# Input rows of the routed expert tiles: gathered and turned by TensorE, or scattered to slots in DRAM and turned by VectorE

## The reference, cut to what matters

```python
def _moe_forward(hidden_states, gate_w, expert_gate, expert_up, expert_down, shared_gate, shared_up, shared_down):
    x = hidden_states.reshape(-1, hdim)                       # 2048 x 512, after a layer norm
    probs = jax.nn.softmax(x @ gate_w.T, axis=-1)             # 8 experts
    routing_weights, selected = jax.lax.top_k(probs, 2)
    routing_weights = routing_weights / (routing_weights.sum(axis=-1, keepdims=True) + 1e-20)
    combine = ...                                             # 2048 x 8, two entries a row
    out = jax.nn.silu(x @ shared_gate.T) * (x @ shared_up.T) @ shared_down.T
    g = jnp.einsum('nh,eih->nei', x, expert_gate)             # i = 352
    u = jnp.einsum('nh,eih->nei', x, expert_up)
    y = jnp.einsum('nei,ehi->neh', jax.nn.silu(g) * u, expert_down)
    return out + jnp.einsum('neh,ne->nh', y, combine)
```

## Time and profile before

| | us |
|---|---|
| median of 3 runs | 1586.21 |
| lowest and highest | 1584.1, 1586.29 |
| span of the profiled execution | 1583.3 |

### The profile page before, as it was taken

One profiled execution on the slowest core, in us unless ns is written; L12 is line 12 of the kernel. 1 busy time (PEld: TensorE's weight loads), 2 busy tenths in 40 slices (PEclk: granted clock), 3 DMA queues, 4 the chain that ended last, 5 costly groups with the idle time before them and its releaser, 6 DMA issues.

```text
span 1583.3 us, 23811 instructions
## 1 busy us (share of the span) xinstructions
PE 1556.1 (98%) x7776; PEld 1332.6 (84%) x7777; DVE 1040.8 (66%) x2230; ACT 583.5 (37%) x997; POOL 455.2 (29%) x390
## 2 busy tenths in 40 slices
PE   7999999999999999999999999999999999999996
PEld 5888888888888888888888888888888889999995
DVE  4798877788887788787787778755663582222221
ACT  4444443434444434444344344333111322333332
POOL 3445332134223233222233221113200003332342
PEclk9999999999999999999999999999999999999998
DMA  7886764677976686985686777466631037778743
GB/s 288 280 315 221 231 220 138 236 289 263 307 278 225 249 307 242 305 302 211 247 308 248 298 295 277 138 212 194 235 100 48 7 114 217 233 194 264 220 86 40
DMA packets 106004, 351.70 MB, mean 222 GB/s; under 512 B 11248, under 2 KB 31728, under 8 KB 100400
## 3 DMA queue, kind: packets, MB, share of 16 engines
q1 hardware_dynamic: 92688, 312.63, 54.9%
q0 software_dynamic: 13216, 37.79, 10.2%
HBM read 227.18 MB, written 123.19 MB: 221 GB/s over the span
## 4 chain that ended last, share of the span: by engine, by line
PE 93%; DVE 3%; DMA 1%; POOL 1%; issue 1%; ACT 1%; POOLq 0%; SPq 0%; ACTq 0%; DVEq 0%
PE bank L366 30%; PE bank L368 30%; PE bank L367 30%; PE bank L1956 1%; PE bank L2075 1%; DMA rows<-x_rows,ids_e 0%; DMA resid<-x 0%; POOL store L669 0%; PE bank L2032 0%; DMA out<-x_early,ids_e 0%; DVE place_hot L1638 0%; DVE tile_vals L1648 0%; DVE resid L1476 0%; PE bank L1756 0%; PE bank L1755 0%
## 5 line engine op out<-in xcount | busy, mean ns | idle before, releaser
L711 POOL TENSOR_TENSOR probs<-probs,causal 128x256 f32<-128x256 f32 x126 | 90.7, 740 | 408.5 <-ACT probs L891 408.5
L368 PE MATMUL bank<-store,wqk 128*128 128x512 f32 x512 | 202.1, 395 | 0.0
L367 PE MATMUL bank<-store,wqk 128*128 128x512 f32 x512 | 201.8, 394 | 0.0
L366 PE MATMUL bank<-store,wqk 128*128 128x512 f32 x512 | 201.8, 394 | 0.0
L1284 DVE SCALAR_TENSOR_TENSOR resid<-bank,factor,resid 128x512 f32<-128x512 f32 x256 | 189.3, 741 | 1.2 <-PE bank L368 1.1
L669 POOL TENSOR_TENSOR pre_split<-pre_raw,pre_split 128x1528 fp32r<-128x1528 f32 x34 | 120.7, 3550 | 142.4 <-ACT pre_split L853 142.4
L889 ACT ACTIVATE probs<-bank 128x512 f32<-128x512 f32 x189 | 85.8, 528 | 131.2 <-PE bank L368 131.2
L368 PEld LDWEIGHTS bank<-store,wqk 128*128 128x128 f32 x512 | 96.0, 188 | 22.9
L367 PEld LDWEIGHTS bank<-store,wqk 128*128 128x128 f32 x512 | 96.0, 188 | 20.8
L366 PEld LDWEIGHTS bank<-store,wqk 128*128 128x128 f32 x512 | 96.0, 188 | 20.0 <-DMA wqk<-wqk_parts 0.2
L1315 DVE TRANSPOSE_TENSOR_REDUCE bank<-probs 128x16 f32<-128x512 f32 (+3 forms) x256 | 108.4, 492 | 0.0
(11 more groups left out here) (333 smaller groups left out, 3966.9 us busy)
## 6 DMA issues: line engine op xcount, KB each, us to landing
pre_parts<-pre_split SPq DMA_DIRECT2D x34, 1528.0 KB, 6.6
wqk<-wqk_parts SPq DMA_DIRECT2D x96, 512.0 KB, 5.0
pre_raw<-pre SPq DMA_DIRECT2D x34, 764.0 KB, 8.0
store<-wv_parts SPq DMA_DIRECT2D x12, 2048.0 KB, 9.4
wo<-wo_parts SPq DMA_DIRECT2D x48, 512.0 KB, 8.3
expert_w<-pre_parts SPq DMA_DIRECT2D x8, 2816.0 KB, 11.6
wqk_parts<-wqk SPq DMA_DIRECT2D x16, 1024.0 KB, 5.1
expert_w<-pre_parts SPq DMA_DIRECT2D x8, 1536.0 KB, 8.8
```

Source lines behind the costliest of these rows:

```text
L366: nc.tensor.matmul(out_ap, a_hi, b_hi, start=first, stop=False)
L367: nc.tensor.matmul(out_ap, a_hi, b_lo, start=False, stop=False)
L368: return nc.tensor.matmul(out_ap, a_lo, b_hi, start=False, stop=last)
L711: nc.gpsimd.tensor_tensor(diagonal, diagonal, causal[:, :, :], ALU.mult).then_inc(S["masked"], 1)
```

## The change

- A new DRAM tensor `es` holds the 39 tiles in slot order. It is filled with zeros by SP in five pieces of up to 2 MB in the attention units 7 to 11.
- As soon as `slot_e` is there, POOL scatters the layer-normed rows of all 16 tiles to their two slots, 32 indirect DMAs (`scatter_e`). Their source is SBUF: SP first reloads the rows from `x3_rows` into `resid` (whose own tiles have been stored by then) and a new buffer `staging`, in four loads (`stage`).
- The first six tiles of the routed stage are gathered by row number as before, `gather(0)` to `gather(3)` after 22 of the scatters, `gather(4)` and `gather(5)` after 26.
- Tiles 6 to 38 are loaded from `es` by four DMAs of 64 KB each, issued by ScalarE in step `g-4` between `y_copy_e` and `aT_high`. VectorE turns tile `g` in step `g-2`, between `xT_low` and `aT_low`. TensorE no longer transposes them.
- The weight loads wait for the end of the up and of the down product (`e_up`, `e_y`) instead of for the transposes that follow them.

```diff
-        E_ROWS, E_AHEAD = 4, 6
+        E_ROWS, E_GATHERED, E_LOADS = 4, 6, 4
+        STAGED = ((0, 6), (6, 10), (10, 13), (13, 16))
+        GATHERS_FROM, MORE_GATHERS = 11, 13
...
-            fills = [(xs, "zero_filled_x", at) for at in range(0, XTILES, ZTILES)]
+            fills = [(xs, "zero_filled_x", at) for at in range(0, XTILES, ZTILES)] + [(es, "zero_filled_e", at) for at in range(0, ETILES, 2 * ZTILES)]
...
-                for part, used, lo, n in (("up", "e_xT_ready", 0, UP), ("down", "e_aT_ready", UP, DOWN)):
+                for part, used, lo, n in (("up", "e_up", 0, UP), ("down", "e_y", UP, DOWN)):
...
-                        sp.wait_ge(S[used], tiles_before + 1)
+                        sp.wait_ge(S[used], tiles_before)
...
+            def stage(n):
+                lo, hi = STAGED[n]
+                to = staging[:, :, :] if n == 1 else resid[:, lo % 10:lo % 10 + hi - lo, :]
+                sp.dma_start(to, x3_rows[lo * P:hi * P].rearrange("(t p) d -> p t d", p=P)).then_inc(S[f"x_tile{n}"], 16)
...
+            def scatter_e(t):
+                if t in dict(STAGED):
+                    pool.wait_ge(S[f"x_tile{[lo for lo, _ in STAGED].index(t)}"], 32)
+                for c in range(TOPK):
+                    nc.gpsimd.indirect_dma_start(es, bass.IndirectOffsetOnAxis(slot_e[:, c, t:t + 1], 0), staged(t), None).then_inc(scat[min(t // 3, 2)], 16)
...
-            pool.wait_ge(S["ids_ready"], 1)
-            for g in range(E_AHEAD):
-                gather(g)
+            pool.wait_ge(S["slots_ready"], TOPK)
+            for t in range(TILES):
+                if t == GATHERS_FROM:
+                    pool.wait_ge(S["ids_ready"], 1)
+                    for g in range(E_ROWS):
+                        gather(g)
+                if t == MORE_GATHERS:
+                    for g in range(E_ROWS, E_GATHERED):
+                        gather(g)
+                scatter_e(t)
             pool.wait_ge(S["stored"], 16 * TILES)
             for g in range(ETILES):
-                if g + E_AHEAD < ETILES:
-                    gather(g + E_AHEAD)
                 add_rows(g)
...
+            def load_turned_e(g):
+                if g == E_GATHERED:
+                    for n, tiles in enumerate((3, 3, TILES - 6)):
+                        act.wait_ge(scat[n], SCAT_X + 16 * TOPK * tiles)
+                if g >= E_GATHERED + E_ROWS:
+                    act.wait_ge(S["e_xT_ready"], g - E_ROWS + 1)
+                if g >= E_GATHERED + 2:
+                    act.wait_ge(S[f"x3_turned{g % 2}"], TURNED_X3 + 16 * QUADS * ((g - E_GATHERED) // 2))
+                load_turned(resid[:, g % E_ROWS, :], es[g * P:g * P + P], S[f"x3_turned{g % 2}"], nc.scalar)
...
+            def turn_e(g):
+                dve.wait_ge(S["e_xT_lo"], g)
+                dve.wait_ge(S[f"x3_turned{g % 2}"], TURNED_X3 + 16 * QUADS * ((g - E_GATHERED) // 2 + 1))
+                turn(resid[:, g % E_ROWS, :]).then_inc(S["e_xT_ready"], 1)
...
-                    transpose_rows_e(i, j + 1)
+                    if rows_next:
+                        transpose_rows_e(i, j + 1)
```

More of the change, by code:

```diff
@@ L154, in build, with staged @@
         tile_vals = sb("tile_vals", [P, TOPK * TILES, 3 * ETABLE], F32R)
+        staging = sb("staging", [P, 4, D])
+        assert sb.at <= second_region + 4 * 2 * KC * SH_WIDTH
+        def staged(t):
+            return staging[:, t - 6, :] if 6 <= t < 10 else resid[:, t % 10, :]
         NE = EXPERTS * TILES
@@ L340, in build @@
         SH_PIECES = 2 * (2 * KC + 4)
-        E_ROWS, E_AHEAD = 4, 6
+        E_ROWS, E_GATHERED, E_LOADS = 4, 6, 4
+        STAGED = ((0, 6), (6, 10), (10, 13), (13, 16))
+        GATHERS_FROM, MORE_GATHERS = 11, 13
+        SCAT_X = 16 * BATCH
+        TURNED_X3 = 16 * 4 * (TILES - TURNED_FROM) // 2
         LAST_PARTS = ((0, SEQ), (SEQ, SEQ), (2 * SEQ, 2 * P))
@@ L374, in every, with load_turned @@
             return row.rearrange("p (m k) -> p k m", k=KC)[:, k, :]
-        def load_turned(tile, source, done):
+        def load_turned(tile, source, done, engine=nc.sync):
             for r in range(QUADS):
-                nc.sync.dma_start(tile[r * BLOCK:(r + 1) * BLOCK, :].rearrange("x (a q) -> x a q", a=QUADS),
+                engine.dma_start(tile[r * BLOCK:(r + 1) * BLOCK, :].rearrange("x (a q) -> x a q", a=QUADS),
                                   source[:, r * P:(r + 1) * P].rearrange("(a x) q -> x a q", x=BLOCK)).then_inc(done, 16)
@@ L546, in _ @@
                     rows_of, done, at = fills[u - 2]
-                    fill(rows_of, done, at, min(ZTILES, rows_of.shape[0] // P - at))
+                    fill(rows_of, done, at, min(ZTILES if done == "zero_filled_x" else 2 * ZTILES, rows_of.shape[0] // P - at))
                 if u == 2 + len(fills):
@@ L560, in _ @@
                     load_ct(1)
-            sp.wait_ge(S["zero_filled_x"], 16 * len(fills))
+            sp.wait_ge(S["zero_filled_x"], 16 * -(-XTILES // ZTILES))
+            sp.wait_ge(S["zero_filled_e"], 16 * -(-ETILES // (2 * ZTILES)))
             def load_row(ph, source, g, j):
@@ L644, in _ @@
             turn_x3(TILES - 1)
+            def stage(n):
+                lo, hi = STAGED[n]
+                to = staging[:, :, :] if n == 1 else resid[:, lo % 10:lo % 10 + hi - lo, :]
+                sp.dma_start(to, x3_rows[lo * P:hi * P].rearrange("(t p) d -> p t d", p=P)).then_inc(S[f"x_tile{n}"], 16)
             for t in range(TILES):
+                if t == 6:
+                    for j in range(2):
+                        sp.wait_ge(S[f"x3_stored{j}"], 16 * (TILES // 2))
+                    sp.wait_ge(S["stored"], 16 * t)
+                    stage(0)
+                    sp.wait_ge(S["s_up"], 2 * TILES)
+                    stage(1)
+                if t == 11:
+                    sp.wait_ge(scat[0], SCAT_X + 16 * TOPK * 3)
+                    stage(2)
+                if t == 12:
+                    sp.wait_ge(scat[1], SCAT_X + 16 * TOPK * 3)
+                    stage(3)
                 if t == TILES - 2:
@@ L1020, in step_e @@
                         y_copy_e(g - 1)
+                if E_GATHERED <= g + E_LOADS < ETILES:
+                    load_turned_e(g + E_LOADS)
                 if g == 0:
@@ L1163, in route_slots @@
                 link(nc.vector.tensor_reduce(w.slot_f[:, :], w.above[:, 0:NE].rearrange("p (e t) -> p t e", e=EXPERTS), mybir.AxisListType.X, ALU.add))
-                link(nc.vector.tensor_copy(slot_e[:, c, :], w.slot_f[:, :]))
+                nc.vector.tensor_copy(slot_e[:, c, :], w.slot_f[:, :]).then_inc(S["slots_ready"], 1)
+                dve.wait_ge(S["slots_ready"], c + 1)
             def route_tiles(w, tiles, tile_expert):
@@ L1490, in step @@
                     shared_add(TILES - 1)
+                if ph == "e" and E_GATHERED <= g + 2 < ETILES:
+                    turn_e(g + 2)
                 if between:
@@ L2076, in transpose_rows_e, with e_step @@
                 last.then_inc(S["e_xT_ready"], 1)
-            def e_step(i, j, first=False, second=True):
+            def e_step(i, j, first=False, second=True, rows_next=False):
                 g = 4 * i + j
@@ L2120, in _ @@
             pe.wait_ge(S["s_y_out"], TILES)
-            e_step(0, 1, second=False)
-            by_fours(pe, e_step, 2, ETILES - 2)
+            e_step(0, 1, second=False, rows_next=True)
+            for g in range(2, E_GATHERED - 1):
+                e_step(g // 4, g % 4, rows_next=True)
+            by_fours(pe, e_step, E_GATHERED - 1, ETILES - 2)
             last = ETILES - 1
-            transpose_rows_e(last // 4, last % 4)
             e_down(last - 2, place(last - 2), True)
```

4 lines of the change are left out of this document (3 added, 1 removed).

## The result

The changed kernel took **1607.31 us** (1605.94 to 1609.27), against 1586.25 before in the same comparison: a ratio of 1.0138, interval 1.0127 to 1.015. It is slower by 1.4%. The forecast was 1590, with a range up to 1604. The profiled execution has a span of 1607.2, 23.9 above that of before.

A forecast was written before the change was run, and what follows sets the result against it. TensorE, busy for 98% of the span, was taken as the bound. On a span of 1583.3: +6.9 front, +3.5 clock, -15.5 transposes, +9.0 late loads gives 1587.2; plus 2.9 to the median, 1590 us, range 1577 to 1604.

The forecast's parts named there:

- the chain of adds: Routed stage: each add waits for the last one's landing; no term in the sum, only a rival of chance 0.13.
- The gain on TensorE: Tiles 6 to 38: four row transposes leave each of 33 steps, 6.74 to 6.27 us, -15.5 us in all.
- The front: Start of the routed stage: 22 scatters ahead of the first gather make row 0 late, +6.9 us, ends 4.1 and 10.
- The issue: Front: after 22 scatters at 1.27 us each, gather 0 goes out at 1301.3, 4.1 us later than before.
- The landing: Front: gather 0, under expert 1's weights, lands 8.5 us after its issue, against 5.71 before.
- The clock: Front: TensorE idles some 7 us and its granted clock drops, +3.5 us, bounds 0 and 4.
- The loads against the weights: Six weight pairs in the routed stage: turned loads land 1.5 us late in each, +9 us, ends 0 and 24.
- rival A: Routed stage: turned loads are in time, perhaps through several pieces per engine turn; 1581 us, chance 0.28.
- 32 turns x 17.5 / 32: Turned load beside a weight pair: its 32 pieces per engine alternate with weight packets over the pair's 17.5 us.
- ScalarE's issues: Routed steps: four DMA issues at 0.45 to 0.67 us each, nothing on the path; rival if over 0.74, chance 0.10.
- Rival B: End of the routed stage: the chain of adds, each awaiting the last landing, sets the end; 1586 to 1591, chance 0.13.
- The median: Whole kernel: the measured median lies 2.9 us above the profiled execution's span, so 1587.2 becomes 1590 us.

The follow-up runs named there:

- e1: The changed kernel with its adds going in turn to three tensors, two thirds of the results left out of the output: 1591.83 us.
- e17: The changed kernel with scatters spread and 14 tiles gathered as in e14, weights unpaced, adds to three tensors (two thirds of results left out): 1570.94 us.
- e11: The changed kernel with ten tiles gathered, gathers 0 to 3 after 14 scatters, expert 1's weights after the scatters, later weights over three steps: 1601.58 us.
- e3: The changed kernel with only an eighth of the weights of experts 2 to 7 loaded, results wrong: 1607.3 us.
- e13: e11 with the 32 scatters writing only the first 16 of a row's 512 floats, to another tensor, results wrong: 1600.64 us.
- e14: The changed kernel, 14 tiles gathered, at most 16 scatters before the first add, others behind adds 0 to 7, later weights over three steps: 1582.68 us.
- e5: The changed kernel with every expert weight load issued as four, each a quarter of the columns, same bytes: 1610.21 us.
- e9: The changed kernel with the weights of experts 2 to 7 spread over three steps, same bytes: 1600.98 us.
- e16: e14 with the later weights spread over four steps instead of three: 1579.36 us.

## Why the prediction was wrong

**The step that failed: the chain of adds stood in the sum at nothing.** The sum took it as running beside TensorE. By the profiled spans, the front took 17.3 us up to the second add (10.4 forecast), 33 steps that are 0.50 shorter would give 16.5 (15.5 forecast), the turned loads cost nothing (9 forecast), and the chain of adds, with the stalls that it causes, takes what remains: 23.9 - 17.3 + 16.5 = 23.1 us (nothing forecast). e1 puts it at 25 and e17 at 26.7. The terms one by one:

**The gain on TensorE: right.** Steps of 6.24 where it isn't held up (e1, e17); I had 6.27.

**The front: right in kind, half the size.** I had +6.9 for row 0; it was 15.7. Two terms failed. The issue: 1301.3 forecast, 1306.0 measured, since the scatters are not 0.97 us each while VectorE works on the routing tables. POOL's timeline of the changed kernel at the start of them:

```profile
1273.08 1.06 POOL L831 DMA_INDIRECT es<-resid,slot_e  x1 [104.63 <-DVE slot_e L1221]
1274.45 0.97 POOL L831 DMA_INDIRECT es<-resid,slot_e  x1 [0.30 <-issue]
1275.72 2.10 POOL L831 DMA_INDIRECT es<-resid,slot_e  x1 [0.30 <-issue]
1278.13 0.96 POOL L831 DMA_INDIRECT es<-resid,slot_e  x1 [0.30 <-issue]
1279.40 2.60 POOL L831 DMA_INDIRECT es<-resid,slot_e  x1 [0.30 <-issue]
```

Six of the first twelve took 1.2 to 2.6 us, and none of the later ones did; VectorE was busy for 35.24 of the 40 us from 1260. The Trainium skill, "SBUF — State Buffer", section "SBUF: two separate sides", says that GpSimd can't write the descriptors of its DMAs while VectorE holds the port pair that they share; the rows fit that, though no run here took VectorE's work away. My row for the price was from a stretch with less work on VectorE. The landing: 8.5 forecast, 12.66 measured. From 1306 to 1318.8 POOL's queue moved 1.85 MB, where the two gathers issued then are 0.52, beside 3.52 MB of SP's. So the queued scatters ahead of the gather count as well as the weights beside it; I had put that into the bound ("three us more") and not into the middle. The bound of 10 for both together was too low.

**The clock: right in kind, half the size.** +3.5 forecast, a size that no row or run shows. From the transposes of tile 0 (15.7 late) to the second add (17.3 late) another 1.6 us were lost, at a granted clock of 0.66 and 0.92.

**The loads against the weights: wrong, and the largest of the forecast's costs.** +9 forecast, 0 measured. The sharing was as I had it. DMA queues from 1418 to 1420, the weights (q1), an add (q0) and a turned load (q10); packets, MB, share of 16 engines:

```profile
q1 hardware_dynamic: 51, 0.57, 71.0%
q0 software_dynamic: 51, 0.10, 29.9%
q10 hardware_dynamic: 51, 0.03, 6.1%
```

These counts are one packet each in turn, whatever its size. The rule of rival A, many pieces at a turn, isn't borne out. What I missed is that a pair isn't one stream. The second load is issued when the down product is through, here at 1418.5 (in the trace of before at 1406.2, where I had read about 1405). The first load's packets end at about 1420.6, the second's begin at about 1421.4, and the queued pieces run through the hole between them. From 1421 to 1422:

```profile
q10 hardware_dynamic: 527, 0.24, 82.7%
q1 hardware_dynamic: 23, 0.11, 27.2%
q0 software_dynamic: 15, 0.01, 7.9%
```

A whole tile's worth, 527 pieces, in one microsecond. The tile issued at 1412.3 had its last piece 9.3 us later, where I had 16.5 and a limit of 15. What failed in this term is "32 turns x 17.5 / 32": the last turns cost nothing.

**ScalarE's issues: right.** 0.45 to 0.67 forecast, 1.76 / 4 = 0.44 measured in most steps, hidden. The price isn't fixed: it reached 2.32 / 4 = 0.58 here and 4.29 / 4 = 1.07 in a step of e11, and e3 showed what the issues cost when they aren't hidden.

**Rival B was the case, and its place was wrong.** I had the chain of adds set the end only, as something that runs beside TensorE, from 1328, with 36 us for the pairs, and gave it 0.13 and 1586 to 1591. It started at 1336.9. The pairs cost more: 261.4 - 38 x 5.65 = 46.7 us above the undisturbed pace. And a late chain doesn't only end late. The four buffers hold ScalarE, which holds TensorE, which then loses clock too: TensorE's last result left PSUM at about 1584, 13 us later than before, and the last add was another 10.7 us further behind it. I had written down the slack (1.1 us a step before, 0.6 after) and not asked whether six losses of 5 to 10 us could be paid back out of it. Between two pairs there are four to five steps (27 us from 1370.06 to 1397.02 in the trace of before, four steps). At 1.1 us a step they pay back 4 to 5 us, at 0.6 no more than 3. The numbers were in my rows; that comparison would have put the chain into the sum.

**The median.** I added 2.9 us for the distance of span and median; here it was 0.1.

Left open: why ScalarE, and at times TensorE, stand for 3 to 25 us with their inputs ready while POOL issues scatters one after another (e1 and e3 to e11, e13), and why the changed kernel's own profiled execution shows none of these waits and comes out at nearly the same time. e13 excludes the scatters' bytes, and with the scatters spread (e14) the waits are down to 4.8 us and less; no run shows a mechanism, and e14 differs from e13 in the gathered tiles and in expert 1's weights too. So the front's cost is shown to come with the crowd of scatters, and how it arises only in part. A wait only where an expert ends, which the adds allow (a row occurs once in an expert's tiles), was not tried: POOL would have to wait on a register's value.

## What to carry to other kernels

When a step gets shorter, list every chain that runs beside it with its own pace and its own disturbances, and ask whether the slack that is left still pays for them between two disturbances; buffers turn a late side chain into a stall of the main engine. Large loads beside a serial chain were best issued in pieces over the steps that they had, not as soon as their buffer was free. A burst of indirect DMAs was cheaper here spread in the waits of a queue than ahead of its first use.

## What the runs showed that I had not expected

An add beside weights isn't slow from its first byte on; it starts late. The add issued at 1411.15 had its first packet at about 1416, where an undisturbed one has it about 2 us after its issue. Until then the weights had the engines alone (1412 to 1416):

```profile
q1 hardware_dynamic: 129, 1.45, 90.0%
q10 hardware_dynamic: 1, 0.00, 0.0%
```

Only then do the turns of one packet each begin. It was the same with quarters (e5): the add issued at 1412.68 had its first three packets in the microsecond from 1417, after the weights had moved 1.41 MB alone from 1413. So I read it that what counts is how much a load has put ahead of the add; this fits that quarters of the packet size changed nothing and that less weight in a step did (e9, e14, e16), and no run tests it alone. Four DMA issues of ScalarE took 1.76 to 2.32 us in the changed kernel, but 2.7 to 4.3 in some steps of e3, e9, e11, e14, e16 and e17; why is not known.
